# A fused Mamba and mixture-of-experts kernel: the last two blocks as expert groups of their own, late blocks combined two per iteration

## The reference

```python
# part 1, a Mamba layer
xn = layernorm(x)
x_ssm, z = split(xn @ in_proj_w.T)                 # 512 + 512
xc = silu(causal_conv(x_ssm, 4 taps) + conv_b)
B, C, dt = xc @ x_proj_w.T                         # 16, 16, 1; dt = softplus
h[t] = exp(dt * A) * h[t-1] + dt * B[t] * xc[t]    # state 512 x 16, scan over time
y = sum_n h[:, n] * C[n] + D * xc
x1 = x + (y * silu(z)) @ out_proj_w.T
# part 2, a mixture of 8 experts, the best 2 for each token
w, e = top2(softmax(layernorm(x1) @ router_w.T + router_b))
out = x1 + sum_k w_k * (layernorm(x1) @ expert_weights[e_k])
```

## Time and profile before

| | us |
|---|---|
| median of 3 runs (lowest, highest) | 3035.31 (3031.69, 3042.91) |
| the profiled execution | 3033.59 |
| its span, first to last instruction | 3031.7 |
| PE, DVE, POOL, ACT busy in it | 2435.8, 2314.1, 1810.3, 1435.6 |

### The profile page before, as it was taken

One profiled execution on the slowest core, in us unless ns is written; L12 is line 12 of the kernel. 1 busy time (PEld: TensorE's weight loads), 2 busy tenths in 40 slices (PEclk: granted clock), 3 DMA queues, 4 the chain that ended last, 5 costly groups with the idle time before them and its releaser, 6 DMA issues.

```text
span 3031.7 us, 35667 instructions
## 1 busy us (share of the span) xinstructions
PE 2435.8 (80%) x10000; PEld 1466.7 (48%) x10000; DVE 2314.1 (76%) x3233; ACT 1435.6 (47%) x2386; POOL 1810.3 (60%) x1418
## 2 busy tenths in 40 slices
PE   5677777798979899798979898797979898778770
PEld 3344444454545555455545554554545454544330
DVE  1788998988888888888888887888888888881000
ACT  2453546354555546354545546464545555342220
POOL 0555666556566757567676767577666767572223
PEclk9777777799989999898979999899989899888895
DMA  1773432223234434334334444344334444343665
GB/s 58 260 253 102 140 125 80 87 81 114 77 102 115 129 112 129 108 115 132 108 112 119 126 122 131 110 117 131 107 114 121 129 115 126 105 144 110 175 173 109
DMA packets 195502, 373.16 MB, mean 123 GB/s; under 512 B 23024, under 2 KB 23024, under 8 KB 195312
## 3 DMA queue, kind: packets, MB, share of 16 engines
q1 hardware_dynamic: 146576, 263.91, 27.1%
q0 software_dynamic: 28672, 67.13, 10.5%
q10 hardware_dynamic: 20064, 39.85, 3.6%
HBM read 212.99 MB, written 157.81 MB: 122 GB/s over the span
## 4 chain that ended last, share of the span: by engine, by line
PE 38%; DVE 19%; issue 16%; POOL 11%; ACT 9%; DMA 5%; SPq 1%; DVEq 0%; POOLq 0%; ACTq 0%
PE work L992 28%; DVE h L817 7%; POOL u L560 6%; PE hT L997 6%; DVE acc L832 6%; ACT decay L694 2%; DVE xc L850 2%; PE work L997 2%; DMA x_out<-result_scratch,rows_of 2%; POOL x_out L661 1%; PE work L1046 1%; ACT L694 1%; POOL row_scratch L645 1%; POOL row_scratch L647 1%; ACT xc L730 1%
## 5 line engine op out<-in xcount | busy, mean ns | idle before, releaser
L560 POOL TENSOR_TENSOR u<-xc,b_ring 128x1024 f32<-128x1024 f32 x512 | 1230.8, 2416 | 778.8 <-DVE h L817 424.2
L694 ACT ACTIVATE decay<-dt,neg_a 128x512 f32<-128x512 f32 x1024 | 699.7, 689 | 680.4 <-DVE h L817 671.3
L997 PE MATMUL hT<-ident,h 128*128 128x128 f32 x4096 | 680.7, 305 | 320.9 <-DVE acc L832 173.4
L997 PEld LDWEIGHTS hT<-ident,h 128*128 128x128 f32 x4096 | 530.4, 157 | 573.6 <-DVE acc L832 246.9
L832 DVE SCALAR_TENSOR_TENSOR acc<-hT,ct,acc 128x512 f32<-128x512 f32 x960 | 700.2, 730 | 134.1 <-PE hT L997 132.5
L992 PE MATMUL work<-w_exp,xeT 128*128 x1536 | 721.1, 614 | 34.1 <-ACT xeT L784 15.5
L817 DVE TENSOR_TENSOR_SCAN h<-decay,h_last,u 128x512 f32<-128x512 f32 x512 | 653.0, 1275 | 90.7 <-ACT decay L694 66.7
L817 DVE TENSOR_TENSOR_SCAN h<-decay,u 128x512 f32<-128x512 f32 x512 | 621.5, 1214 | 106.6 <-ACT decay L694 92.3
L992 PE MATMUL work<-xnT,w_in 128*128 128x512 f32 x1024 | 469.2, 602 | 0.8 <-ACT xnT L709 0.8
L992 PEld LDWEIGHTS work<-w_exp,xeT 128*128 128x128 f32 x1536 | 286.7, 195 | 361.8 <-issue 360.5
L661 POOL DMA_INDIRECT x_out<-result_scratch,rows_of x128 | 205.8, 1608 | 189.6 <-DMA x_out<-x_scratch 100.2
(11 more groups left out here) (140 smaller groups left out, 1892.5 us busy)
## 6 DMA issues: line engine op xcount, KB each, us to landing
b_ring<-b_scratch SPq DMA_DIRECT2D x256, 256.0 KB, 3.9
xe<-row_scratch SPq DMA_DIRECT2D x180, 256.0 KB
result_scratch<-ye SPq DMA_DIRECT2D x180, 256.0 KB
row_scratch<-x_out ACTq DMA_DIRECT2D x32, 1024.0 KB, 5.0
xn<-in_x SPq DMA_DIRECT2D x64, 256.0 KB, 4.6
x<-in_x SPq DMA_DIRECT2D x64, 256.0 KB, 4.3
x_scratch<-x SPq DMA_DIRECT2D x64, 256.0 KB, 4.4
x_out<-x_scratch SPq DMA_DIRECT2D x64, 256.0 KB, 3.3
```

Of the source, the lines that this page charges most:

```text
L560: nc.gpsimd.tensor_tensor(out=u[:, at:at + 2, :], in0=xc[:, half, 2 * k:2 * k + 2, :], in1=b_ring[:, n % ROWS:n % ROWS + 1, :].to_broadcas ...
L694: nc.scalar.activation(decay_bank[g % 2][:], dt[:, half, :], ACT.Exp, scale=neg_a[:, c, n:n + 1]).then_inc(decay_ready, 1)
L997: last = nc.tensor.transpose(ps[:, k * P:(k + 1) * P], tile(k), ident[:])
```

## The change

The blocks are cut into groups: seven pairs (0,1) to (12,13), as before, and blocks 14 and 15 alone. A group has at most `TOP*Q*n + 7` tiles, 23 for a pair and 15 for a single block. Iterations 3 to 14 hold 12 and 11 tiles of groups 0 to 5 in turn, iteration 15 all 23 of group 6, iterations 16 and 17 the 15 of groups 7 and 8. Blocks up to 9 are combined as before, 10 and 11 in iteration 15, 12 and 13 in 16, 14 in 17 and 15 in 18, which is the last. From iteration 15 on odd tiles use the second buffers. `tile_row` and `tile_expert` have two buffers, the results two tensors, and the clearing of results is gone. Block 15 is combined in `x1`, which has a buffer for each q. `LAG` is 1. All slots are new; the tables of iterations 15 and 16 (`EXPERTS_LATE`, `EXPERTS_END`, 23 and 15 tiles) are new as well.

```diff
-    XT = TOP * SQ + E
-    HALF_XT = XT // 2
+    GROUPS = [(b, 2) for b in range(0, BLOCKS - 2, 2)] + [(BLOCKS - 2, 1), (BLOCKS - 1, 1)]
+    TILES = [TOP * Q * n + E - 1 for first, n in GROUPS]
+    XT = max(TILES)
+    for g in range(len(GROUPS) - 3):
+        EXPERT_PLAN[2 * g + 3] = (g, 0, XT - XT // 2)
+        EXPERT_PLAN[2 * g + 4] = (g, XT - XT // 2, XT // 2)
+    for i in range(3):
+        g = len(GROUPS) - 3 + i
+        EXPERT_PLAN[BLOCKS - 1 + i] = (g, 0, TILES[g])
+    COMBINE_PLAN = {j: [j - 5] for j in range(5, BLOCKS - 1)}
+    COMBINE_PLAN[BLOCKS - 1] = [BLOCKS - 6, BLOCKS - 5]
+    COMBINE_PLAN[BLOCKS] = [BLOCKS - 4, BLOCKS - 3]
+    COMBINE_PLAN[BLOCKS + 1] = [BLOCKS - 2]
+    COMBINE_PLAN[BLOCKS + 2] = [BLOCKS - 1]
+    NEW_GROUP = {first + n + 1: g for g, (first, n) in enumerate(GROUPS)}
-    LAG = 0
+    LAG = 1
     COMBINE = {
-        "fetch": [6.43, 26.69, 31.82, 46.2],
-        "gather": [17.4, 21.01, 29.67, 35.48, 50.48, 55, 59.51, 66.9],
-        "store": [20.79, 36.24, 56.3, 66.9],
+        "fetch": [0.6, 21.84, 27.83, 42.12],
+        "gather": [22.9, 25.23, 34.74, 37.3, 53.04, 56.5, 66.3, 66.3],
+        "store": [22.36, 37.96, 57.96, 66.42],
     }
...
+    def combine_in(j):
+        blocks = len(COMBINE_PLAN.get(j, []))
+        return [((at + i * N * C) / blocks, (kind, i * Q + s[0]) + tuple(s[1:])) for i in range(blocks) for at, (kind, *s) in steps_in(COMBINE)]
-    def closing_steps(j, first):
+    def closing_steps(j):
+        if j == BLOCKS + 2:
+            return ([("gather", q, 0) for q in range(Q)] + [("gather", q, 1) for q in range(Q)] + [("store", q) for q in range(Q)])
...
-        fetch = [[("fetch", q), ("gather", q, 0), ("gather", q, 1)] for q in range(Q)] + [[]]
-        rows = [fetch[0]] + [[fetch[q + 1], [("store", q)]] for q in range(Q)]
-        rows[1:] = [sum(x, []) for x in rows[1:]]
-        steps = list(first)
-        for i in range(1 + HALF_XT):
-            steps += tiles[i] if j <= BLOCKS + 2 else []
-            steps += rows[i // 3] if i % 3 == 0 else []
+        rows = [[("fetch", q), ("gather", q, 0), ("gather", q, 1), ("store", q)] for q in range(Q)] + [[("fetch_last", q) for q in range(Q)]]
+        steps = [("new_group", 0)]
+        for i, tile in enumerate(tiles):
+            steps += tile
+            steps += rows[i // 3] if i % 3 == 0 and i // 3 < len(rows) else []
         return steps
...
+        if j in NEW_GROUP:
+            side = [(6, ("new_group", 0))] + side
-            side = side + [(8 * i + 1, ("zero_results", i)) for i in range(RESULT_ZEROS)]
...
+        def late(tile):
+            return TILE_STEP[tile][0] >= BLOCKS - 1 and tile % 2 == 1
+        def xe_of(tile):
+            return xn[:, 0, :] if late(tile) else xe[:]
...
+                    elif s[0] == "fetch_last":
+                        q = s[1]
+                        sync.wait_ge(scattered[q], 16 * BLOCKS)
+                        sync.wait_ge(x1_stored[q], 16 * BLOCKS)
+                        first = (BLOCKS - 1) * T + q * P
+                        sync.dma_start(x1[:, q, :], x1_dram[first:first + P, :]).then_inc(res_loaded[q], 16)
...
+                        if g >= 3:
+                            for k in range(2):
+                                dve.wait_ge(gathered[k], 16 * TOP * Q // 2 * GROUPS[g - 2][0])
+                        link(nc.vector.tensor_copy(rows_of[g % 3][:], result_f[:]))
+                        if g >= 2:
+                            done_tiles(dve, rows_stored, FIRST_TILE[g - 1])
```

More of the change, by code:

```diff
@@ L41, in mamba_moe_kernel @@
     HT = 2
-    LAG = 0
-    ROW_ZEROS, RESULT_ZEROS = 32, 6
+    LAG = 1
+    ROW_ZEROS = 32
     COMBINE = {
-        "fetch": [6.43, 26.69, 31.82, 46.2],
-        "gather": [17.4, 21.01, 29.67, 35.48, 50.48, 55, 59.51, 66.9],
-        "store": [20.79, 36.24, 56.3, 66.9],
+        "fetch": [0.6, 21.84, 27.83, 42.12],
+        "gather": [22.9, 25.23, 34.74, 37.3, 53.04, 56.5, 66.3, 66.3],
+        "store": [22.36, 37.96, 57.96, 66.42],
     }
     POST = {
[L51 to L71, removed]
@@ new lines, in mamba_moe_kernel @@
+        "load_res": [6.17, 6.46, 9.42, 15.75],
+        "y_T": [3.26, 3.48, 3.61, 3.79],
+        "y_skip": [4.92, 8.07, 8.63, 9.33],
+        "y_gate": [10.66, 11, 11.06, 11.13],
+        "out_project": [10.7, 12.33, 13.43, 15.85],
+        "residual": [13.63, 15.14, 16.55, 17.72],
+        "rstd2": [19.2, 23.53],
+        "store_x1": [13.64, 16.26, 20.17, 23.25],
+        "norm2": [17.41, 18.97, 23.43, 26.58],
+        "norm2_T": [16.93, 19.21, 23.4, 25.58],
+        "norm2_evict": [18.95, 20.34, 24.92, 27.61],
@@ L95, in mamba_moe_kernel @@
+        "dt_plus": [40.68],
+        "b_scale": [46.21],
+        "b_store": [52.22],
     }
     EXPERTS = {
[L97 to L100, removed]
@@ L186, in work_banks @@
         uses, idle, count, holder = {}, list(range(WORK)), [0] * WORK, {}
-        for j in range(-1, BLOCKS + 5):
+        for j in ITERATIONS:
             for s in iteration(j):
@@ L296, in mamba_moe_kernel @@
         row_f = sb("row_f", [1, XT])
-        tile_row = sb("tile_row", [1, XT], i32)
-        tile_expert = sb("tile_expert", [1, XT], i32)
+        tile_row = [sb(f"tile_row{i}", [1, XT], i32) for i in range(2)]
+        tile_expert = [sb(f"tile_expert{i}", [1, XT], i32) for i in range(2)]
         xe = sb("xe", [P, D])
@@ L394, in wait, with ye_of, same_buffer, tile_of @@
                 eng.wait_ge(s, value)
[L396 to L403, removed]
+        def late(tile):
+            return TILE_STEP[tile][0] >= BLOCKS - 1 and tile % 2 == 1
+        def xe_of(tile):
+            return xn[:, 0, :] if late(tile) else xe[:]
+        def ye_of(tile):
+            return xn[:, 1, :] if late(tile) else ye[:]
+        def same_buffer(tile):
+            return max((t for t in range(tile) if late(t) == late(tile)), default=None)
+        def tile_of(j, i):
+            g, lo, _ = EXPERT_PLAN[j]
+            return g, lo + i, FIRST_TILE[g] + lo + i
+        def done_tiles(eng, sems, tiles):
+            for k in range(2):
+                wait(eng, sems[k], 16 * ((tiles - k + 1) // 2))
         def wait_full(eng, j, key):
@@ L486, in steps_of @@
-                        sync.dma_start(xe_of(j, i), row_dram[bass.ds(row, P), :]).then_inc(rows_loaded[i % 2], 16)
+                        row = sync.value_load(tile_row[g % 2][0:1, at:at + 1], min_val=0, max_val=2 * REGION - P)
+                        sync.dma_start(xe_of(tile), row_dram[bass.ds(row, P), :]).then_inc(rows_loaded[tile % 2], 16)
                     elif s[0] == "rows_store":
-                        i = s[1]
-                        wait_used(sync, j, ("expert", i))
-                        at = i + (1 - half) * HALF_XT
@@ L491, in steps_of @@
-                        first = (pair + half) % 2 * RESULTS + at * P
-                        sync.dma_start(res_dram[first:first + P, :], ye_of(j, i)).then_inc(rows_stored[i % 2], 16)
-                    elif s[0] == "fetch":
+                        g, at, tile = tile_of(j, s[1])
+                        wait_used(sync, j, ("expert", s[1]))
+                        sync.dma_start(res_dram[g % 2][at * P:(at + 1) * P, :], ye_of(tile)).then_inc(rows_stored[tile % 2], 16)
+                    elif s[0] == "fetch":
+                        block, q = COMBINE_PLAN[j][s[1] // Q], s[1] % Q
+                        wait(sync, stored[q % 2], 16 * (2 * block + q // 2))
+                        sync.wait_ge(x1_stored[q], 16 * (block + 1))
+                        first = block * T + q * P
+                        sync.dma_start(x_out[:, q % 2, :], x1_dram[first:first + P, :]).then_inc(x_out_loaded[q % 2], 16)
+                    elif s[0] == "fetch_last":
@@ L596, in steps_of @@
                     elif s[0] == "gate_weights":
-                        first = (1 - half) * Q
-                        tiles = slice(first, first + Q)
-                        parity = 1 - half
-                        before, after = mask_before[parity], mask_before[1 - parity][:, 0, :] if parity == 0 else mask_total[:]
+                        g, pos = GROUP_OF[r]
+                        tiles = slice(pos * Q, pos * Q + Q)
+                        before, after = mask_before[pos], mask_total[:] if pos == GROUPS[g][1] - 1 else mask_before[pos + 1][:, 0, :]
                         count = [0]
```

343 lines of the change are left out of this document (182 added, 161 removed).

## The result

The changed kernel takes 3135.8 us (median of 5, 3123.6 to 3139.9) against 3035.3: ratio 1.032, interval 1.030 to 1.035. It is slower, outside the range and against the forecast sign.

A forecast was written before the change was run, and what follows sets the result against it. PE and DVE, neither full, were taken to bound the kernel by handing work to each other. 3031.7 + 31 + 8 - 4 - 58 - 12 - 6 = 2990.7 us of span, given as 2995 us; range 2930 to 3045.

The forecast's parts named there:

- forecast sign: Whole kernel: faster, by 1.3%.
- (a): Iteration 15: 23 tiles instead of 12 and a second block combined, +31 us, between +10 and +60.
- (b): Iteration 16: 15 tiles instead of 12, a group table and eight gathers more, +8 us, between -10 and +30.
- (c): Iteration 17: 15 tiles instead of 24, but SP stands at stores and PE idles, -4 us, between -53 and +10.
- (d): The end after the last result store: 23.3 us instead of 81.4, -58 us, between -45 and -60.
- (e): Iterations 3 to 14: 6 tiles fewer, half of their PE time on the path, -12 us, between -23 and 0.
- (f): Sums one slot later (LAG 1), all places new: the tight place moves, -6 us, between -65 and +60.
- rival 4: Slower, as the scan now waits for the last transpose: +69 us, 3064 us in all, chance 0.10.

The follow-up runs named there:

- e4: e2 with each combine store in iteration 17 issued three tiles after its gathers: 2972.6 us, ratio 0.978.
- e2: The changed kernel with LAG 0 and, before iteration 15, the four slot tables of the kernel before: 3017.3 us, ratio 0.994.
- e3: e2 with LAG 1, and y_T and y_skip one slot later before iteration 15: 3123.0 us, ratio 1.028.
- e7: e2 with only y_T and y_skip one slot later before iteration 15, LAG still 0: 3058.7 us, ratio 1.008.
- e5: e2 with only the transposes one slot later, the sums as at LAG 0: 3108.7 us, ratio 1.024.
- e6: e2 with only the sums one slot later, transposes as at LAG 0, and y_T and y_skip one slot later: 3496.0 us, ratio 1.151.
- e9: e4 with the old COMBINE slots, halved, in iterations 15 and 16 too: 2986.4 us, ratio 0.983.

## Why the prediction was wrong

By its own steps, against the table of stretches:

- (a) +31: measured +31.3. The sum is right, its split less so: PE's busy time rose by 34.4 us where 38.6 were put, and PE is still idle 29.6 us of 180.5 (32.7 before) where 20.5 and 4 were put. That the two errors cancel is luck.
- (b) +8: +15.5, inside its bounds. The last group's first load went out 1.4 us after the store ahead of it instead of 5.6, as forecast. What made the 7.5 us is not shown; POOL stood 31.7 us in eight places for the first gather of a pair, against 10.2 in three before. The gap of 9.41 us, which the second buffers were to take away, is the start of iteration 17 in the rows and not one of iteration 16.
- (c) -4: +1.1. Right in mechanism (50.3 us of SP at the stores, a cycle of 24.5 us for three tiles where 22.6 was worked out) and shown by e4, which takes only this away. One reading in it is wrong: SP did not stand for the 14.4 us from 2840.84 to 2855.27 in the kernel before. It issued seven other DMAs in between, and the store came late because it stands three tiles later in the list. In the changed kernel a fetch and its store are 12.7 to 13.4 us apart, so the figure taken came near by luck.
- (d) -58: -57.4. Right.
- (e) -12: e2 gives -16, the four others with its iterations -6 to -10. Right, as far as 10 us can be told apart.
- (f) -6, bounds -65 and +60: this is the step that failed. With (e) it came to +100.4, so (f) is +117 against e2 and +106 against the slowest of its kin, nearly twice its upper bound. The whole span was missed by 130.8 us (2990.7 against 3121.5), and 118 of them are (e) and (f) together.

What (f) said was that the tight place only moves, from the first sum to the scan after next, and that a scan's wait for the transpose bounds the price. e3 shows that the scan does wait there (66.7 us), as rival 4 had it. But in the changed kernel this wait is only 24.6 us, and rival 4's price, 3064, is 72 us short: it had the sign for a reason that carries little of the loss. The larger row is PE waiting before transposes, 75 us more in twelve iterations, which the working left out. Two counts were wrong. Moving the transposes with the sums takes away the one slot of four without a transpose, in which PE had room for a product of 3.6 us; I counted slack on DVE's side only and not where the products stand between. And the first transpose of a group was given 4.0 us of slack, although its bank is freed by a sum that LAG 1 puts behind the scan. These two are argued from the lists and the waits. The bound of +60 does not follow from its own words either: a wait at the scan as long as the one at the sums now is 8.6 us an iteration, 129 in fifteen, and that would have held what was measured.

The second error is of the same step: "all places new" was priced together with LAG as one small number. The experiments show that they are not additive. Stretch 0-15 is 2467 with old slots and LAG 0, 2579 with old and LAG 1, 2584 with new and LAG 1, 2651 with new and LAG 0. LAG 1 costs 112 with the old slots (with the `y` steps, see e7) and gives 67 back with the new; under LAG 1 the two sets of slots are equal within the noise.

One cost of the new slots can be seen in DVE's own busy time, which is 2184.2 us in this stretch against 2145.3 in e2 and 2157.8 in e3. Small instructions stand much longer, e2's two rows first and then the changed kernel's:

```profile
L1036 DVE TENSOR_TENSOR picked_row<-pick,rank_row 128x32 f32<-128x32 f32 x28 | 4.1, 189 | 0.5
...
L1041 DVE CAST row_at<-row_f 128x8 uint32<-128x8 f32 x14 | 2.4, 172 | 0.5
```

```profile
L977 DVE TENSOR_TENSOR picked_row<-pick,rank_row 128x32 f32<-128x32 f32 x28 | 20.7, 779 | 0.5
L982 DVE CAST row_at<-row_f 128x8 uint32<-128x8 f32 x14 | 11.9, 848 | 0.5
```

The long ones end when a product of `u` ends on POOL, here at 1900.7 us on both:

```profile
1896.02 4.66 POOL L619 TENSOR_TENSOR u<-xc,b_ring 128x1024 f32<-128x1024 f32 x2
...
1896.34 4.38 DVE L977 TENSOR_TENSOR picked_row<-pick,rank_row 128x32 f32<-128x32 f32 x2
```

These two groups take 26 us more than in e2, in a list in which DVE's next steps stand behind them. With e3's old slots they take 6.5 us in all, as in e2. Nothing was run to tell how much of the time they cost.

Shown is thus: the loss goes with LAG 1 and the slots that came with it, e2 against the changed kernel; with the old slots LAG 1 and the `y` steps it needs are enough for one as large, e3; both halves of LAG 1 cost when alone, e5 and e6; the groups, the plan of the tail and the tensors cost nothing in this stretch. Not settled is which of the new slots make 2651 out of 2467 at LAG 0; no table was exchanged alone. That the missing free slot of PE is the cause within LAG 1 is argued from e3's and e5's waits; a third bank for transposes, which would test it, was not tried.

The best version is the change without its LAG and new slots for full iterations, with the store moved: 2972.6 us, 62.8 less than before. Its profile against before: stretch 0-15 -6, iteration 15 +36, iteration 16 +16, the closing tiles -45, the end -57.

## What to carry over

Price a change piece by piece even when it arrives as one: here a good tail (-57 at its end, -46 more with one step moved) was buried under an order of the steady part that cost 106 to 117. In this software pipeline the order is fitted as a whole. A shift of one slot changes nothing in the work and cost from 2.7 us (e7) to 29 us (e6) an iteration, fifteen times, so its upper bound isn't the wait seen now. And in a list that one engine walks in order, don't put the wait for a long chain right behind the start of that chain: that was the 46 us of e4.

## What the runs showed that was not expected

- With two transpose banks, sums one slot later without the transposes cost 437 us (e6 against e7), the largest effect of any edit; PE's granted clock fell to 0.83 and its busy time in the stretch rose from 2075.6 to 2279.8 us for the same products.
- The old combine slots, with more distance between the two gathers of a pair, made iteration 16 longer by 9.5 us (e9 against e4).
- Small DVE instructions of 0.2 us took up to 2.4 us while POOL was in a product of `u`, and ended with it: 26 us more in two groups of the changed kernel than in e2.
- Iterations 0 to 14 of the same instructions in the same order took 2467.0 to 2477.2 us in five profiled executions, so one profile's sum of a long stretch is good to some 10 us.
